# Reordering the attention rounds of a fused pre-norm block: first loads, K's head sums, a sum of squares, the second norm's statistics, the input's low halves

## What is computed

```python
q, k, v = (silu(causal_conv4(x @ W)) for W in (Wq, Wk, Wv))   # 4 heads of 64
q, k = q / norm(q), k / norm(k)
beta = sigmoid(x @ Wb);  Kb, Vb = K * beta, V * beta          # chunks of 64 tokens
T = inverse of (I + tril(Kb K^T, -1)), by forward substitution
W, U = T @ Kb, T @ Vb
# scan over chunks with state S; only its diagonal Sd enters the outputs
u = U - W * Sd;  o = q * Sd + tril(sum(q * k)) * u;  S = S + K^T u
o = o * rsqrt(mean(o * o) + eps) * g;  attn = o @ Wo
# ffn: 2 shared experts for all tokens, plus the best 2 of 8 routed experts, GELU between two matmuls
```

## Time and profile before

| | us |
|---|---|
| median of 3 runs (1258.93 to 1262.52) | 1259.58 |
| the profiled execution, time | 1258.96 |
| its span, first to last instruction | 1257.2 |
| TensorE busy | 1129.3 (90%) |
| VectorE busy | 697.4 (55%) |
| ScalarE busy | 622.1 (49%) |
| GpSimd busy | 381.2 (30%) |

### The profile page before, as it was taken

The page is one execution under the profiler, slowest core; times in us unless marked ns, Lnnn a source line. Parts: engine busy times, 40 slices in busy tenths (PEclk is TensorE's granted clock), DMA queues, the critical chain, the costliest instruction groups (busy, mean ns, idle before and its releaser), DMA issues.

```text
span 1257.2 us, 25606 instructions
## 1 busy us (share of the span) xinstructions
PE 1129.3 (90%) x9320; PEld 969.5 (77%) x9321; DVE 697.4 (55%) x1203; ACT 622.1 (49%) x1117; POOL 381.2 (30%) x328
## 2 busy tenths in 40 slices
PE   2696979998989899987898889999999999999997
PEld 1365768777777778876777778899998999999986
DVE  2767766666766666556679842333333333333377
ACT  2665545656574754562654553344444444444442
POOL 0325352534343322522101201343344334433100
PEclk9888878999998999997999999999999999999998
DMA  3112020202020110334413321111111111111456
GB/s 128 32 53 67 1 76 1 76 10 76 1 84 1 38 31 9 127 119 143 135 43 108 111 85 52 43 47 47 51 50 46 46 50 46 50 55 42 150 192 226
DMA packets 54088, 86.36 MB, mean 69 GB/s; under 512 B 6656, under 2 KB 39296, under 8 KB 53888
## 3 DMA queue, kind: packets, MB, share of 16 engines
q1 hardware_dynamic: 46336, 64.37, 15.9%
q0 software_dynamic: 7680, 20.98, 5.4%
HBM read 60.16 MB, written 25.17 MB: 68 GB/s over the span
## 4 chain that ended last, share of the span: by engine, by line
PE 69%; DVE 18%; ACT 7%; issue 3%; POOL 2%; DMA 1%; SPq 0%; DVEq 0%; ACTq 0%; POOLq 0%
PE ps L1379 25%; PE ps L1359 23%; DVE W L1537 4%; PE ps L1216 4%; PE ps L1206 3%; PE ps L1370 3%; PE ps L1278 2%; PE ps L1285 2%; DVE late_room L1719 2%; PE ps L1437 2%; DVE W L1629 1%; PE ps L1339 1%; POOL W L813 1%; PE ps L1321 1%; DVE W L1887 1%
## 5 line engine op out<-in xcount | busy, mean ns | idle before, releaser
L1359 PE MATMUL ps<-late_room,W 128*128 128x256 f16 x3072 | 359.1, 276 | 27.4 <-DVE late_room L1719 21.2
L1379 PE MATMUL ps<-W,late_room 128*128 (+1 forms) x3264 | 379.4, 277 | 0.0
L1379 PEld LDWEIGHTS ps<-W,late_room 128*128 128x128 f16 x3264 | 324.8, 100 | 42.8
L1359 PEld LDWEIGHTS ps<-late_room,W 128*128 (+1 forms) x3072 | 301.7, 99 | 71.2 <-DVE late_room L1719 26.7
L1082 ACT ACTIVATE ps<-ps 128x512 f32<-128x512 f32 x272 | 158.7, 583 | 355.9 <-PE ps L1359 316.5
L1719 DVE SCALAR_TENSOR_TENSOR late_room<-ps,late_room 128x512 f16<-128x512 f32 x272 | 181.0, 687 | 235.2 <-ACT late_room L1087 220.1
L1087 ACT ACTIVATE late_room<-ps 128x512 f16<-128x512 f32 x272 | 155.7, 595 | 2.5
L1537 DVE SCALAR_TENSOR_TENSOR W<-W 128x512 f32<-128x512 f32 x144 | 122.2, 849 | 9.3 <-ACT W L955 5.9
L1216 PE MATMUL ps<-W 128*128 128x512 f16 x384 | 102.3, 412 | 1.5 <-DVE W L1713 1.5
L936 ACT COPY W<-ps 128x512 f32<-128x512 f32 x112 | 61.1, 589 | 45.2 <-PE ps L1278 33.8
L1959 DVE TENSOR_SCALAR late_room<-ps 128x512 f32<-128x512 f32 x36 | 24.9, 691 | 97.8 <-PE ps L1379 97.8
(11 more groups left out here) (188 smaller groups left out, 1362.5 us busy)
## 6 DMA issues: line engine op xcount, KB each, us to landing
wstage<-in_w_ffn SPq DMA_DIRECT2D x40, 512.0 KB, 3.6
W<-yt_d SPq DMA_DIRECT2D x16, 512.0 KB, 5.9
late_room<-in_x SPq DMA_DIRECT2D x8, 512.0 KB, 4.7
W<-in_x SPq DMA_DIRECT2D x8, 512.0 KB, 4.1
x2n_d<-W SPq DMA_DIRECT2D x8, 512.0 KB, 3.2
base_d<-W SPq DMA_DIRECT2D x8, 512.0 KB, 3.7
late_room<-base_d SPq DMA_DIRECT2D x16, 256.0 KB, 4.3
acc_d<-late_room SPq DMA_DIRECT2D x12, 256.0 KB
```

The lines of the kernel that those rows point to most:

```text
L1359: last = pe.matmul(up_bank(n, c)[:, f * XT:(f + 1) * XT], weight(slot, d, hw, cols), x_halves[:, hx, d], start=(q == 0), stop=(q == len(pa ...
L1379: last = pe.matmul(down_bank(b)[:, c * D:(c + 1) * D], hs[b][:, hh, f, c * P:(c + 1) * P], weight(slot, DB + f // 4, hw, cols), start=(q = ...
```

## The change

Five things move. (1) The identity is loaded first, then the projection weights, each with a semaphore of its own, then the other eight constants. TensorE waits first for the identity alone, ScalarE for the weights; VectorE's preparation of weights becomes `prepare()`, behind the first group's statistics (end of slot 6, round 0). (2) TensorE does `project(0)` in slot 4, ahead of K's head sums; ScalarE empties `proj0` before `ssq`, and copies `ssq` in slot 5; GpSimd's powers move one slot later. (3) The sum `osqT + qsqT` (128x1024) moves from GpSimd's slot 3 to VectorE's slot 4. (4) The second norm's statistics are taken of tiles 0 and 1 right after their residual is added (slot 8), of tiles 2 and 3 at the end of slot 9, behind L1570, L1573 and L1719; ScalarE's second normalisation stands behind X and the high half `xnT1` in slot 11, the first one at the end of slot 8, behind the first GELU and high half. (5) The low halves of the next input (L1713) move from slots 10 and 11 to the ends of slots 9 and 10, so the first of them stands ahead of `nmr2`. With that, the routed pieces split in round 10 (`EARLY_AT`) move from slots 1, 3, ... 15 to 4, 5, 6, 7, 10, 11, 13, 15.

```diff
-CONSTS_IN = 16 * 10
+CONSTS_IN = 16 * 8
-EARLY_AT = {(slot, t): (SLOTS_A // 2) * (t - GROUPS - 1) + slot // 2
-            for t in (GROUPS + 1, GROUPS + 2) for slot in range(1, SLOTS_A, 2)}
+EARLY_AT = {(2 * q + 1, GROUPS + 1): q for q in range(SLOTS_A // 2)}
+EARLY_AT |= {(slot, GROUPS + 2): SLOTS_A // 2 + q for q, slot in enumerate((4, 5, 6, 7, 10, 11, 13, 15))}
 FRONT_FILLS = (
-    [(f"proj{m}", "act") for m in PROJ_ORDER[:6]]
-    + [("ssq", "act"), (f"proj{PROJ_ORDER[6]}", "act")]
+    [(f"proj{m}", "act") for m in PROJ_ORDER[:7]]
+    + [("ssq", "act")]
...
-            for dst, src in ((wp_stage, w_proj), (cw, conv_w), (idt[:], ident), (masks, lvl_masks),
-                             (minus2i, eye2), (wo, w_o), (gcol, g_col), (cen, cent), (headsel, head_sel),
-                             (headones, head_ones)):
+            sp.dma_start(idt[:], ident).then_inc(ident_in, 16)
+            sp.dma_start(wp_stage, w_proj).then_inc(proj_in, 16)
+            for dst, src in ((cw, conv_w), (headsel, head_sel), (masks, lvl_masks), (minus2i, eye2),
+                             (headones, head_ones), (wo, w_o), (gcol, g_col), (cen, cent)):
                 sp.dma_start(dst, src).then_inc(const_in, 16)
...
-                if slot == 3:
-
-                    pool.wait_ge(q_sq, DB * (n + 1))
-                    pool.wait_ge(o_own_sq, DB * (n + 1))
-                    pool.tensor_tensor(osqT, osqT, qsqT, ALU.add).then_inc(o_sq, 1)
...
             act.wait_ge(consts_made, CONSTS_MADE)
-            act.wait_ge(const_in, CONSTS_IN)
-
+            act.wait_ge(proj_in, 16)
...
                 if slot == 4:
                     silu(3)
                     project(5)
+                    if n >= 2:
+
+                        act.wait_ge(o_ready, n - 1)
+                    project(0)
+                if slot == 5:
                     act.wait_ge(*fr.full(n, "ssq"))
                     act.copy(ssq, fr.bank("ssq")[:, 0:GT * NH]).then_inc(fr.empty(n, "ssq")[0], 1)
...
+            def behind(slot, t):
+                if slot == 11 and 0 <= t - 3 < GROUPS:
+                    normalise_out(t - 3, (t - 3) % BATCH)
...
             def extras(slot, t):
+                if slot == 8 and t < GROUPS:
+                    normalise(t)
...
-            pe.wait_ge(consts_made, CONSTS_MADE)
-            pe.wait_ge(const_in, CONSTS_IN)
+            pe.wait_ge(ident_in, 16)
...
                 if slot == 4:
                     project(5)
-
+                    project(0)
+                    if not n:
+
+                        pe.wait_ge(const_in, CONSTS_IN)
+                        pe.wait_ge(consts_made, CONSTS_MADE)
                     pe.wait_ge(squares, DB * (n + 1))
                     head_sums(fill(fr, n, "ssq"), sqK).then_inc(fr.sem_full, 1)
                 if slot == 5:
-                    project(0)
                     turn_out(fr, n, "tokK0", Kr, 0)
...
+                if slot == 4:
+
+                    dve.wait_ge(q_sq, DB * (n + 1))
+                    dve.wait_ge(o_own_sq, DB * (n + 1))
+                    dve.tensor_tensor(osqT, osqT, qsqT, ALU.add).then_inc(o_sq, 1)
...
                         dve.tensor_tensor(part, part, tl.bank(name), ALU.add).then_inc(tl.empty(n, name)[0], 1)
-                if slot == 9:
-                    dve.wait_ge(*tl.empty(n, "attn1"))
-                    layer_stats(n, xr, bn2, mv2, rstd2, stats2)
+                        if h == 0:
+                            dve.wait_ge(*tl.empty(n, name))
+                            tile_stats(xr, bn2, (0, 1), stats2)
...
             def extras(slot, t):
+                if (slot, t) == (6, 0):
+                    prepare()
+                if slot == 9 and 0 <= t - 3 < GROUPS:
+                    dve.wait_ge(*tl.empty(t - 3, "attn1"))
+                    tile_stats(xr, bn2, (2, 3), stats2)
+                    joined_stats(t - 3, bn2, mv2, rstd2, stats2)
+                if slot in (9, 10) and t < GROUPS:
+                    xnT_low(slot - 9, t)
                 split_piece(slot, t)
```

More of the change, by code:

```diff
@@ L293, with run_attention @@
 SCATTER_LAG = 4
-def run_attention(front, back, tail, ahead, down=None, up=None, extra=None, lead=False):
+def run_attention(front, back, tail, ahead, down=None, up=None, behind=None, extra=None, lead=False):
     for t in range(GROUPS + 4):
@@ L304, in run_attention @@
             fed = ((down, t - 5, FED), (up, t - 4, FED))
-            for stage, n, last in (fed + own if lead else own + fed):
+            for stage, n, last in (fed + own if lead else own):
+                if stage and 0 <= n < last:
+                    stage(slot, n, n % BATCH)
+            if behind:
+                behind(slot, t)
+            for stage, n, last in (() if lead else fed):
                 if stage and 0 <= n < last:
@@ L964, in front @@
                 if slot == 0:
+                    if not n:
+                        act.wait_ge(wp_low, DB + 1)
                     if n >= 2:
@@ L993, in front @@
                     project(0)
+                if slot == 5:
+                    act.wait_ge(*fr.full(n, "ssq"))
+                    act.copy(ssq, fr.bank("ssq")[:, 0:GT * NH]).then_inc(fr.empty(n, "ssq")[0], 1)
                     silu(4)
@@ L1063, in tail, with normalise_out, normalise @@
                     act.activation(xs[n % 2][:, 0], x2nT[:, :, 0:XT], ACT.Copy, scale=X_SCALE).then_inc(fed_high, 1)
-            def ahead(slot, n, b):
-                if slot == 8:
-                    act.wait_ge(nmr_ready, n + 1)
-                    if n:
-                        act.wait_ge(*fr.full(n - 1, "tokK1"))
-                        act.wait_ge(*ah.full(n - 1, "xnT1"))
-                    for k in range(GT):
-                        act.activation(xn[:, k], xl[:, k], ACT.Identity, bias=nmr[:, k:k + 1],
-                                       scale=rstd[:, k:k + 1]).then_inc(xn_ready, 1)
+            def normalise_out(n, b):
+                act.wait_ge(nmr2_ready, n + 1)
+                if n:
+                    act.wait_ge(base_ready, n)
+                    act.wait_ge(tokens_out[1 - b], 32 * ((n + 1) // 2))
+                for k in range(GT):
+                    act.activation(x2n[:, k], xr[:, k], ACT.Identity, bias=nmr2[:, k:k + 1],
+                                   scale=rstd2[:, k:k + 1]).then_inc(x2n_ready, 1)
+            def normalise(n):
+                act.wait_ge(nmr_ready, n + 1)
+                if n:
+                    act.wait_ge(*fr.full(n - 1, "tokK1"))
+                    act.wait_ge(*ah.full(n - 1, "xnT1"))
+                for k in range(GT):
+                    act.activation(xn[:, k], xl[:, k], ACT.Identity, bias=nmr[:, k:k + 1],
+                                   scale=rstd[:, k:k + 1]).then_inc(xn_ready, 1)
+            def ahead(slot, n, b):
                 if slot in (10, 11):
@@ L1134, in extras @@
                     act.activation(scr["bl"], scr["z"], ACT.Sigmoid).then_inc(scored, 1)
-            run_attention(front, back, tail, ahead, up=up_piece, extra=extras)
+            run_attention(front, back, tail, ahead, up=up_piece, behind=behind, extra=extras)
             def x_high_half(t):
@@ L1512, in layer_stats @@
                 last.then_inc(counted, 1)
-                dve.wait_ge(counted, 3 * n + 2)
+                dve.wait_ge(counted, 4 * n + 3)
                 dve.tensor_scalar(rs, m2[:, :, 1], EPS, None, ALU.add).then_inc(counted, 1)
```

63 lines of the change are left out of this document (28 added, 35 removed).

## The result

The changed kernel took 1231.37 us (median of four runs, 1228.1 to 1232.95) beside 1259.26 for the kernel before on the same chip: a ratio of 0.977 (0.974 to 0.979), some 28 us less. The profiled execution (1232.95, the slowest of the four) has a span of 1231.2 us against 1257.2, 26.0 less, at a mean clock of 0.962 against 0.948. The time lies inside the range; the likeliest, 1219, was 12 us too low. It came out near what rivals B (1230) and D (1231) gave, but by neither: the taps were freed and the clock mostly stayed up, and the 12 us were lost at places that the sum had not priced.

What follows compares the result with a forecast made beforehand. TensorE bounds the kernel, with 69% of the chain, through waits and 1.2 GHz stretches. Start 7.7, head-sums wait 13.1, clock 11.3 and second half 8.3 sum to 40.4 us: from 1259.58 to 1219, range 1208 to 1236.

Steps and rivals of the forecast that it cites:

- B: Rival: the clock still falls behind K's head sums and only the wait is gone; 29.1 us won, 1230; chance 0.25.
- D: Rival: VectorE's taps are held up by something that stays, not GpSimd's L833 (the sum); 1231; chance 0.07.
- Start: Before the first projection: weights land at 7.6 us, so it starts at 18.2 instead of 25.95; 7.7 us won.
- K's head sums, wait: Slot 4, TensorE: squares come 1.65 earlier, `project(0)` fills the idle time, which goes whole in round 7; 13.1 us won.
- Clock: Behind K's head sums, rounds 5 to 8: dense projections before them keep the clock up; 11.3 us won, bounds 0 to 22.
- A: Likeliest case: the clock stays up behind K's head sums and all terms hold; 40.4 us won, 1219; chance 0.50.
- Second half: Slots 8 to 11: moved statistics and normalisation cut the L1719 wait; rounds 4 to 8 win 2.4, 1.1, 1.1, 2.2, 0.25.
- the cover of 1.9 us: GpSimd's chain starts 0.6 later, yet what follows ends at 378.0, before TensorE has Z ready at 379.9 (round 6's frame).
- Rival C: Second half gives nothing: late `nmr2` or GpSimd's chain replaces the L1719 wait; 1227, or 1239 with B; chance 0.13.
- the forecast of 8.3: Second-half term in us: 2.4 + 1.1 + 1.1 + 2.2 + 0.25 for rounds 4 to 8, 1.25 for rounds 9 and 10.
- Rounds 9 and 10: Shorter statistics win 0.6 each; in round 10 a piece ahead of L1675 costs about 1.3 back.
- Slower (E): Rival: head sums, Z, `oss` and K's transposes follow closer, so the low clock spreads; 1266 at 6 us a round; chance 0.05.

Runs made afterwards that it cites:

- the three kernels with `nmr2` first: Changed kernel with GpSimd's masked copies held until `nmr2`: alone 1230.66; also first routed piece one slot later, 1230.63; or first two pieces loaded earlier, 1230.93.
- first profile: Profiled execution of the changed kernel in its first measurement, nothing altered: 1232.95 us, the slowest of four runs.
- second profile: Profile of the same changed kernel run once more, nothing altered, beside the kernels with the load earlier: 1231.54 us, ratio 0.978.

## Why the prediction was right or wrong

**Start: right.** 8.0 us for 7.7. Some 2 us of it were lost in round 1 (5.8 and 6.2 left at the first Y of round 2, where 7.4 was expected). The new order of `project(0)` can cost that much there: alone, with no change at the start, it made the first Y of round 2 2.0 us later (65.22 for 63.20). But with parts 1 to 3 together 6.4 and 7.2 were left, so it is not the same in each execution, and I have not taken it apart.

**K's head sums, wait: the mechanism right, the size too large.** In slot 3 the taps were held up by the sum on GpSimd and by nothing else: rival D falls with the taps' 2.33 and with the sum alone, worth 20 us. But "head sums start at 394.0 in place of 395.29, the idle 2.60 is gone whole" missed what the new order of the banks brings: 0.72 or 0.77 is left for L959, and head sums start 0.6 to 0.8 earlier, not 1.3. Over rounds 2 and 5 to 8 that is 3.6 us. I had checked when `project(0)`'s bank is free, and not whose bank `ssq` takes.

**Clock: right in kind, by chance in size.** From the head sums to K's second transpose, rounds 3 to 8, 20.9 us were won; less the 7.8 of six `project(0)` moved ahead, 13.1 are clock, where 11.3 was forecast for rounds 5 to 8 alone. In those four rounds there were only 9.9 to win (the stretch against its length at full clock; the chain pieces that the prediction adds up hold some start of a group behind a wait as well, and come to 11.1, not 11.3), and 8.2 of them were won. But A against B was not either-or. Nor is `project(0)` ahead of the head sums needed for it in these rounds, as the prediction had it: the sum alone kept the clock up in three of the four. With an idle time of 0.72 or 0.77 before the head sums, the stretch takes 12.0 us at full clock, or 13.7. Over the nine profiles that have both the sum and `project(0)` moved, it was 13.7 in 13 of the 36 rounds 5 to 8; the kernel before, its `project(0)` taken off, had such an excess in four of four, 1.7 or 3.3 each. Rival B comes true in a third of the rounds. What chooses between them was not tried. Rounds 3 and 4, which I had left as they were, gave 4.9 of the 13.1.

**Second half: the failed step.** Expected 7.05 in rounds 4 to 8; measured 1.05, 0.41, 0.41, 1.52 and -0.53, together 2.9, and -1.11 in round 3, where 0 was expected. What fell is "the power takes 1.01, the first low half fits in that time": I saw that GpSimd is free after the power, and not that it goes straight into L823, which holds up `nmr2` for 0.88 us. The kernel in which GpSimd waits for `nmr2` proves that for 0.37 us a round. The rest of the shortfall of rounds 5 and 6 (1.1 - 0.41 - 0.37 = 0.3 each) I have not taken apart, nor that of rounds 4 and 7. Nor did the cover of 1.9 us before GpSimd's L829 hold: at the first Y of round 9 VectorE waits for it 2.6 us (before 1.3), and the down tile 0.28, in the three kernels with `nmr2` first 1.57. Rival C named both mechanisms, "late behind L1713, or GpSimd's chain, started later"; I gave it 0.13, which was too little, and had it as all or nothing. Parts 4 and 5 gave 1.4 to 1.7 us in each of rounds 5 to 7 against parts 1 to 3 alone, so the slot 11 mechanism itself was right; what the forecast of 8.3 left out is what is given back around it.

**Rounds 9 and 10: wrong.** 0.6 each was expected. Round 9 lost 4.7 us in the first profile and 2.3 in the second. In the first, the piece's load was issued 1.7 us after the round's first Y, where before it was issued 0.6 ahead of it. Of these 2.3 us, 1.4 are the later chain of GpSimd, the residual base L850 (before L845) and its store, behind which the load stands in SyncE's queue; 0.9 are a longer issue just ahead of it, which the second profile does not have. I had followed GpSimd's chain to the scan, and not to SyncE's queue behind it. In the second profile the load cost 0.06 us, and most of the loss is the clock, which kernels without parts 4 and 5 lost in this round too. How much of round 9 belongs to these parts stays open. In round 10 `oss` came 2.1 us earlier and 2.1 were lost again behind it: 1.4 are there when VectorE reaches L1703 (before L1675), with a piece ahead of it, where I had 1.3; the other 0.7 come later in the round, with the other pieces and the statistics on VectorE, and were not taken apart.

**Slower (E): did not happen.** Head sums, Z, `oss` and the transposes follow closer on each other, and TensorE's down matmuls between them run in 2.78 us in most rounds.

## What to carry to other kernels

When a step is moved, look at what the engine that makes its input does next: freed early, GpSimd starts its following long instruction, and a tiny instruction of VectorE right behind pays for it. When one matmul group takes over another's bank, the new wait is for whoever empties that bank. Compare a part with the kernel that lacks only that part: against the kernel before, parts 4 and 5 seemed to give 0.4 us in round 6, against parts 1 to 3 alone they gave 1.7. And two profiles of one program can differ by 3 to 5 us, because the clock falls behind the same wait in one and not in the other; an edit priced under that needs a mechanism seen in its rows, and many runs for its worth.

## What the runs showed of the hardware

- A VectorE instruction on 128x4 elements took 1.04 us when GpSimd's 128x512 copies had started 0.07 us before it, and 0.16 us when they came after it. The Trainium skill, SBUF — State Buffer, SBUF: two separate sides, calls the shared port pair "an exclusive lock" and gives it to whoever starts first, for the whole instruction. Both numbers agree, and so do the taps, 2.95 us for 0.76 beside the sum. The exception seen before held too: three taps beside GpSimd's power L842 (384.68 to 388.02) took 2.32 us, as without it; there the trace and the page differ.
- The late phase, the same code in all kernels, took from the router of round 10 to the end 645.6, 647.2 or 648.5 us (each within 0.3), and the same kernel showed two of these values: 645.6 in the changed kernel's first profile and 647.2 in its second. What chooses was not tried.
- The same 512 KB piece, in the same place of SyncE's queue, landed 6.9 us after its issue in one profile of the changed kernel and 6.2 in the other, and the transfer issued ahead of it kept SyncE 1.43 us in one and 0.51 in the other. That is 1.6 of the 2.4 us by which it was later in the first.
